# A chain of network blocks on one core: sums turned in 32x32 blocks, q's and k's parts spread in four transfers, gates as rows

## The reference

```python
scores = einsum('bqhd,bkhd->bhqk', q, k) / sqrt(8)
w = softmax(where(mask, -inf, scores), axis=-1)
return einsum('bhqk,bkhd->bqhd', w, v)
```

```python
y = sum_e gate[token, e] * (silu(x @ Wg[e]) * (x @ Wu[e])) @ Wd[e]
```

## Time and profile before

| | us |
|---|---|
| median of 3 runs | 4669.29 |
| the profiled execution, its own time | 4668.61 |
| its span in the trace | 4666.8 |
| PE busy | 4043.2 |
| DVE busy | 3448.4 |
| ACT busy | 2271.0 |

### The profile page before, as it was taken

The page is one execution under the profiler, slowest core; times in us unless marked ns, Lnnn a source line. Parts: engine busy times, 40 slices in busy tenths (PEclk is TensorE's granted clock), DMA queues, the critical chain, the costliest instruction groups (busy, mean ns, idle before and its releaser), DMA issues. The chain is left out here.

```text
span 4666.8 us, 86233 instructions
## 1 busy us (share of the span) xinstructions
PE 4043.2 (87%) x25133; PEld 2627.3 (56%) x25133; DVE 3448.4 (74%) x17477; ACT 2271.0 (49%) x7477; POOL 404.7 (9%) x338
## 2 busy tenths in 40 slices
PE   8999999999999999867888888888887346979897
PEld 6888888888888888642333333333333223534456
DVE  7888888888888888655677777776774557966543
ACT  5555555555555555424555555555555221236432
POOL 0000000000000000011111111111111010024310
PEclk9999999999999999877988888888888567989998
DMA  0000000000000000012122222222220000100001
GB/s 30 2 2 2 2 2 2 2 2 2 2 2 2 2 2 2 21 44 60 33 46 50 49 54 49 53 49 54 49 50 17 8 0 21 35 25 6 8 12 41
DMA packets 79658, 103.76 MB, mean 22 GB/s; under 512 B 25471, under 2 KB 72762, under 8 KB 77243
## 3 DMA queue, kind: packets, MB, share of 16 engines
q1 hardware_dynamic: 79227, 98.70, 8.8%
HBM read 67.60 MB, written 30.26 MB: 21 GB/s over the span
## 5 line engine op out<-in xcount | busy, mean ns | idle before, releaser
L297 DVE CUSTOM_DVE_ANT_0 I-197junk<-I-193encw,I-196expo,I-205rec 128x77 f32<-128x77 f32 x3072 | 945.6, 356 | 7.0
L1328 DVE TENSOR_REDUCE I-41263nmax<-ps 128x1 f32<-128x512 f32 x768 | 501.1, 685 | 223.7 <-PE ps L997 217.3
L1216 ACT ACTIVATE I-41266prob<-ps 128x512 f32<-128x512 f32 x768 | 428.4, 596 | 228.5 <-PE ps L1034 225.8
L275 ACT ACTIVATE I-195tanh_s<-ps 128x77 f32<-128x77 f32 x1024 | 241.3, 236 | 594.9 <-PE ps L255 594.9
L255 PEld LDWEIGHTS ps<-I-190hist,I-49small 128*128 128x128 f32 x2048 | 304.6, 188 | 298.3 <-DVE I-190hist L333 298.3
L255 PE MATMUL ps<-I-190hist,I-49small 128*128 128x77 f32 x2048 | 456.4, 304 | 0.2
L261 PE MATMUL ps<-I-195tanh_s,I-49small 128*128 128x77 f32 x2048 | 454.6, 304 | 0.0
L997 PE MATMUL ps<-I-41257kS,I-41256qS 96*128 96x512 bf16 x768 | 330.9, 457 | 130.3 <-DVE I-41263nmax L1328 58.9
L262 PE MATMUL ps<-I-190hist,I-49small 128*128 128x128 f32 x2048 | 439.5, 296 | 0.0
L257 PE MATMUL ps<-I-190hist,I-194uh_h 128*128 128x128 f32 x2048 | 439.5, 296 | 0.0
L283 ACT ACTIVATE I-201hh<-I-207gate_t,I-206pre,I-200rh 128x1 f32<-128x1 f32 x1024 | 395.5, 386 | 88.1 <-DVE I-206pre L297 0.2
(11 more groups left out here) (531 smaller groups left out, 7286.3 us busy)
## 6 DMA issues: line engine op xcount, KB each, us to landing
I-41256qS<-parts SPq DMA_DIRECT2D x24, 768.0 KB, 7.7
parts<-I-41275room SPq DMA_DIRECT2D x36, 384.0 KB, 2.5
parts<-I-41275room SPq DMA_DIRECT2D x36, 256.0 KB, 2.1
I-41257kS<-parts SPq DMA_DIRECT2D x12, 768.0 KB, 7.9
parts<-I-41275room SPq DMA_DIRECT2D x36, 128.0 KB, 1.8
I-49small<-in_layers SPq DMA_DIRECT2D x6, 768.0 KB, 8.9
I-66556w<-in_blocks SPq DMA_DIRECT2D x8, 514.0 KB, 7.5
I-41256qS<-I-41265mrow SPq DMA_DIRECT2D x192, 2.0 KB
```

The lines of the kernel that those rows point to most:

```text
L297: return e.tensor_tensor_reduce(junk[:, 2 * g + b, :], encw[:, g, b, :], expo[:, b, :], inv[:, b:b + 1], rec[:, b, g:g + 1], ALU.mult, ALU ...
L1216: e.activation(prob[:, tau % 2, j, :], k.ps[:, b, :], ACT.Exp, scale=scale).then_inc(free[b], 1)
L1328: e.tensor_reduce(nmax[:, U % HG, i, j:j + 1], k.ps[:, use[0], :], AX.X, ALU.max, negate=True).then_inc(free[use[0]], 1)
```

## The change

**Sums.** VectorE transposes `inv` in blocks of 32x32 into `wide`, which is free then; a sum that lay in a row of 32 partitions is then in a column of each block. The reciprocal takes these columns alone, 16x3 elements of a partition for groups 0 to 2 and 16x1 for the last, and writes them into the first 64 columns of `inv` (`recs`). In place of each shuffle, a transpose whose source repeats one column 32 times brings the reciprocals back over rows. Cross attention is changed in the same way. There are two more semaphores.

**Transfers.** `spread` issues four transfers for q, k and cq, one for each group of heads, each with a semaphore; ctx keeps one. TensorE waits for group m ahead of that group's first maximum. The next store waits for all four.

**Order.** `TURNS` has new strings for all five engines; the number of steps of each stream is the same.

**Gated experts.** TensorE turns the gates, so that experts are on partitions (68x1024); ScalarE copies them, and SP stores them to DRAM. For each pair SP reads two rows back, each over 64 partitions, into one of three buffers (512 KB per pair). VectorE multiplies the hidden product by this tile. The down projection then takes both experts in one product of 128 rows and sums all pairs in PSUM, in banks 4 and 5; the sum is added once at the end. The silu has two buffers, and no hardware loop is left.

In the diff, removed lines of `gated_experts` are left out (they are printed above), of `TURNS` only the beginning of GpSimd's is shown, and cross attention's part (from L1444 on), which repeats self attention's with `cinv`, `crecs` and `cwide`, is left out.

```diff
 def gated_experts(nc, k, nT, acc, gates, blocks):
     with ExitStack() as ctx:
         w = [sbuf(ctx, nc, f"w{u}", [P, 3 * P]) for u in range(GU)]
+        sil = [sbuf(ctx, nc, f"sil{u}", [P, B * T]) for u in range(2)]
         hid = [sbuf(ctx, nc, f"hid{u}", [P, B * T]) for u in range(2)]
+        spread = [sbuf(ctx, nc, f"spread{u}", [P, B * T]) for u in range(3)]
+        gT = sbuf(ctx, nc, "gT", [2 * NPAIR, B * T])
+        gates_dram = nc.dram_tensor("gates_rows", (2 * NPAIR, B * T), F32).ap()
+        gate, up, total = k.ps[:, 0:2, :], k.ps[:, 2:4, :], k.ps[:, 4:6, :]
+        turned = k.ps[0:2 * NPAIR, 6:8, :]
+        with stage(nc, "turned kept sent gate up act product hidden down summed "
+                       + " ".join(f"load{u}" for u in range(GU)) + " rows0 rows1 rows2") as (block, s):
             load = [s.load0, s.load1, s.load2, s.load3]
+            rows = [s.rows0, s.rows1, s.rows2]
             @block.sync
             def _(e):
+                def fetch(n):
                     e.dma_start(w[n % GU][:], blocks[n]).then_inc(load[n % GU], 16)
+                def fetch_rows(n):
+                    src = gates_dram[2 * n:2 * n + 2, :].unsqueeze(0).to_broadcast([64, 2, B * T])
+                    e.dma_start(spread[n % 3][0:64, :], src[:, 0, :]).then_inc(rows[n % 3], 16)
+                    e.dma_start(spread[n % 3][64:128, :], src[:, 1, :]).then_inc(rows[n % 3], 16)
+                for n in range(GU):
+                    fetch(n)
+                e.wait_ge(s.kept, B)
+                e.dma_start(gates_dram, gT[:]).then_inc(s.sent, 16)
+                e.wait_ge(s.sent, 16)
+                for n in range(3):
+                    fetch_rows(n)
+                for n in range(3, NPAIR):
+                    e.wait_ge(s.hidden, B * (n - 2))
+                    fetch_rows(n)
+                    if n + 1 >= GU and n + 1 < NPAIR:
+                        e.wait_ge(s.down, n + 2 - GU)
+                        fetch(n + 1)
             @block.tensor
             def _(e):
+                for i in range(NT):
+                    mm = e.transpose(turned[:, i // TPB, (i % TPB) * P:(i % TPB + 1) * P], gates[:, i, :], k.ident)
+                    if i % TPB == TPB - 1:
+                        mm.then_inc(s.turned, 1)
+                def hidden(n):
+                    e.wait_ge(load[n % GU], 16 * (n // GU + 1))
                     for b in range(B):
+                        if n:
+                            e.wait_ge(s.act, B * (n - 1) + b + 1)
+                        e.matmul(gate[:, b, :], w[n % GU][:, 0:P], nT[:, b * T:(b + 1) * T], start=True, stop=True).then_inc(s.gate, 1)
+                        if n:
+                            e.wait_ge(s.product, B * (n - 1) + b + 1)
+                        e.matmul(up[:, b, :], w[n % GU][:, P:2 * P], nT[:, b * T:(b + 1) * T], start=True, stop=True).then_inc(s.up, 1)
+                def down(n):
                     for b in range(B):
+                        e.wait_ge(s.hidden, B * n + b + 1)
+                        for i in range(TPB):
+                            mm = e.matmul(total[:, b, i * P:(i + 1) * P], hid[n % 2][:, b * T + i * P:b * T + (i + 1) * P],
+                                          w[n % GU][:, 2 * P:3 * P], start=(n == 0 and i == 0), stop=(n == NPAIR - 1),
+                                          skip_group_check=True)
+                    mm.then_inc(s.down, 1)
+                hidden(0)
+                for n in range(NPAIR):
+                    if n + 1 < NPAIR:
+                        hidden(n + 1)
+                    down(n)
             @block.scalar
             def _(e):
+                for b in range(B):
+                    e.wait_ge(s.turned, b + 1)
+                    e.activation(gT[:, b * T:(b + 1) * T], turned[:, b, :], ACT.Copy).then_inc(s.kept, 1)
+                for n in range(NPAIR):
                     for b in range(B):
+                        e.wait_ge(s.gate, B * n + b + 1)
+                        if n >= 2:
+                            e.wait_ge(s.product, B * (n - 2) + b + 1)
+                        e.activation(sil[n % 2][:, b * T:(b + 1) * T], gate[:, b, :], ACT.Silu).then_inc(s.act, 1)
             @block.vector
             def _(e):
+                for n in range(NPAIR):
                     for b in range(B):
+                        cols = slice(b * T, (b + 1) * T)
+                        e.wait_ge(s.up, B * n + b + 1)
+                        e.wait_ge(s.act, B * n + b + 1)
+                        if n >= 2:
+                            e.wait_ge(s.down, n - 1)
+                        e.tensor_tensor(hid[n % 2][:, cols], sil[n % 2][:, cols], up[:, b, :], ALU.mult).then_inc(s.product, 1)
                     for b in range(B):
+                        cols = slice(b * T, (b + 1) * T)
+                        e.wait_ge(rows[n % 3], 32 * (n // 3 + 1))
+                        e.wait_ge(s.product, B * n + b + 1)
+                        e.tensor_tensor(hid[n % 2][:, cols], hid[n % 2][:, cols], spread[n % 3][:, cols], ALU.mult).then_inc(s.hidden, 1)
@@ TURNS @@
-    gpsimd=("rrrrrrrrrraaarrrrrrrarrrrararrrrrrrrr", "arrrararrrrrrrrrarrrararrrrrrrrr", 3,
...
+    gpsimd=("rrrrrrrrrraaarrrrrrrrrarrarrarrrrrrrrr", "arrarrarrrrrrrrrarrarrarrrrrrrrr", 3,
...
@@ -829,6 +826,7 @@
         crow = sbuf(ctx, nc, "crow", [8, HG, T], BF16)
         cwide = sbuf(ctx, nc, "cwide", [P, 2, T])
         cinv = sbuf(ctx, nc, "cinv", [P, T])
+        recs, crecs = (x[:, 0:HG * T // 32].rearrange("p (b g) -> p b g", g=HG) for x in (inv, cinv))
         room = sbuf(ctx, nc, "room", [P, 8 * T])
         cprob = room[:, 0:4 * T].rearrange("p (j t) -> p j t", t=T)
         flat = room[:, 0:2 * T].rearrange("p (n t) -> p n t", t=T)
@@ -928,6 +926,13 @@
         K_SPOTS = (slice(2, 5), slice(1, 6, 4), slice(0, 1))
         SPOT = dict(ctx=0, cq=1, k=2, q=3)
 
+
+        def sums_of(src, lo, hi):
+            return src.rearrange("p (b q) -> p b q", q=32)[:, :, 8 + lo:8 + hi]
+
+        def along(src, g):
+            return src[:, :, g].unsqueeze(2).to_broadcast([P, T // 32, 32])
+
         def times(r, name):
             return r + 1 if name in ("k", "q") else r - 1
 
@@ -938,9 +943,9 @@
             return chain.from_iterable(part(n) for n in range(NR))
 
         with stage(nc, "full0 full1 full2 full3 full4 full5 full6 full7 free0 free1 free2 free3 free4 free5 free6 free7 "
-                       "high split av pooled inv wide normed sent0 sent1 sent2 sent3 so_in "
+                       "high split av pooled turned inv wide normed sent0 sent1 sent2 sent3 so_in "
                        "stats aggr var rstd shifted norm rotated0 rotated1 jhigh0 jhigh1 rest0 rest1 middle0 middle1 last0 last1 jstored0 jstored1 jstored2 jstored3 "
-                       "jsent0 jsent1 jsent2 jsent3 wk_ready wq_ready chigh csplit csum cinv cwide cnormed "
+                       "jsent0 cq0 cq1 cq2 cq3 k0 k1 k2 k3 q0 q1 q2 q3 wk_ready wq_ready chigh csplit csum cturned cinv cwide cnormed "
                        "csent0 csent1 csent2 csent3 wf_in wk_in wq_in") as (block, s):
             full = [s.full0, s.full1, s.full2, s.full3, s.full4, s.full5, s.full6, s.full7]
             free = [s.free0, s.free1, s.free2, s.free3, s.free4, s.free5, s.free6, s.free7]
@@ -948,7 +953,8 @@
             rotated, jhigh, rest_in, middle, last = zip((s.rotated0, s.jhigh0, s.rest0, s.middle0, s.last0),
                                                         (s.rotated1, s.jhigh1, s.rest1, s.middle1, s.last1))
             jstored = [s.jstored0, s.jstored1, s.jstored2, s.jstored3]
-            jsent = [s.jsent0, s.jsent1, s.jsent2, s.jsent3]
+
+            jsent = dict(ctx=[s.jsent0], cq=[s.cq0, s.cq1, s.cq2, s.cq3], k=[s.k0, s.k1, s.k2, s.k3], q=[s.q0, s.q1, s.q2, s.q3])
             csent = [s.csent0, s.csent1, s.csent2, s.csent3]
 
             def made(use):
@@ -989,9 +995,9 @@
                             if m and n == 2:
                                 turn(U - 1)
                                 yield
-                            if m == 0 and n == 0:
-                                e.wait_ge(s.jsent3, 16 * (a + 1))
-                                e.wait_ge(s.jsent2, 16 * (a + 1))
+                            if n == 0:
+                                e.wait_ge(jsent["q"][m], 16 * (a + 1))
+                                e.wait_ge(jsent["k"][m], 16 * (a + 1))
                             use = M["m", U, i, j]
                             b = open_bank(e, use)
                             e.matmul(k.ps[:, b, :], qS[0:ROWS_QK, c, 4 * m + j, i * P:(i + 1) * P],
@@ -1098,8 +1104,9 @@
                                 if g and i == 2:
                                     turn_cross(g - 1)
                                     yield
+                                if i == 0:
+                                    e.wait_ge(jsent["cq"][g], 16 * times(r, "cq"))
                                 if g == 0 and i == 0:
```

(24 more changed lines are left out.)

170 lines of the change are left out of this document (56 added, 114 removed).

## The result

The changed kernel took 4610.91 us (median of four runs, 4610.72 to 4613.32) where the kernel before took 4669.66 in the same comparison: 58.8 us less, ratio 0.9873 with a 95% interval of 0.9861 to 0.9885. The forecast was 4527, 142 less. The sign, the gated experts and the price of each operation came out; of the transformer's 128 us only some 42 did. The measured time lies at the edge of the wide range (4450 to 4612) and outside the forecast's own (4485 to 4575).

The account below looks back on a forecast made before the run. Dependencies, no full engine, were taken to set the transformer's period; PE and DVE nearly fill the gated experts. 4668.6 - 128.4 - 14.0 = 4526.2 us, 4527 against the median; own range 4485 to 4575, wide range 4450 to 4612.

Parts of the forecast that it names:

- the gated experts: Final stage: a pair falls from 5.61 to 5.22 us and DVE no longer trails, -14.0 us in all.
- the last group's sum: Short stretch of each transformer unit: smaller reciprocal and transposes shorten the last head group's chain, -2.3 us.
- the first unit's term: Transformer's start: the first unit's q transfer has no cover, so its earlier landing gives -5.0 us once.
- cq's landing: Before cross attention's maxima: the first of four transfers lands in 2.7 us, not 7.7, on the chain: -5.0 a unit.
- q's landing: Before self attention's maxima: q lands earlier, but normalisation is the longer chain, so costed at nothing.
- the holes: Long stretch: two cross reciprocals stop PE for 1.3 us each; their removal gives -2.6 us a unit.
- no price of its own: New order of turns, all engines: it only places the shorter work, so it was costed at nothing.
- B: Rival for the split transfers: pieces share the engines and land together, so the split does nothing; 4592, chance 0.22.
- D: Rival in the gated experts: the rows' transfers set the pair at 7.0 us; 4588, chance 0.05.
- C: Rival in the transformer's short stretch: PE's gaps close, clock stays at its upper level, -15.3 per unit; 4462, chance 0.18.
- E: Rival for the sums: block transposes are dear, up to a reciprocal's 3.35 us, making it slower; 4727, chance 0.06.
- F: Rival for the new order: an engine waits at a wrong place and the gain is lost; about 4665, chance 0.04.

Follow-up runs that it names:

- e5: Changed kernel with the old order of turns and one transfer each for k, q and cq: 4647.5 us.
- e1: Changed kernel with the order of turns of the kernel before: 4611.3 us.
- e9: Changed kernel with one transfer each for q, k and cq, and SP's queue alone in its old order: 4647.8 us.
- e7: e1 with cq's join and two remainders made on GpSimd instead of VectorE: 4595.6 us.
- f2: e5 with the next unit's first maxima put behind cq's projections in 8 of 12 units: 4653.3 us.
- g3: e1 with the next unit's first maxima put behind cq's projections in 8 of 12 units: 4643.5 us.
- e2: Kernel before with only the new order of turns: 4766.1 us.
- e8: Changed kernel (new order) with cq's join and two remainders made on GpSimd instead of VectorE: 4589.1 us.
- e4: Changed kernel (new order) with one transfer each for q, k and cq: 4674.2 us.

## Why the prediction was wrong

**Right.** The sign (0.90 on faster), the gated experts (14.0 forecast, 14.6 measured, pair 5.22 forecast and measured), the prices of the new operations, the last group's sum on the path (2.3 shorter: e5 and e1 have the projection done at 4.6 us after the attend, where before has it at 6.8 to 7.3). The first maxima start 5.0 earlier (2139.96 to 2134.92), as the first unit's term says. But most of the gain came from the ends, where I had 9.6: by the ends of attends and of the stage, the first two units gave 15.6, the next nine together 12.8, and what follows 13.6. At the middle's 1.4 a unit, some 25 of the 42 us belong to the ends; no run takes them apart.

**Wrong: cq's landing, -5.0 a unit.** I put it on the chain because the transfer starts at 2606.29 and the cross maxima at 2614.72, 8.4 us later against a landing of 7.7. That was a coincidence of two durations. The row of 2614.72 names no wait for a DMA; it follows maxima of the next unit (2612.93, 2.00 us) that had been held back by DVE. Over the whole run L1107 waited 15.1 us for that DMA (its group stands above), and in the steady part from 2459 to 3197 not once. The two were close, though: cq landed 0.3 to 1.3 us ahead of its use, so a shorter landing had nothing to win while DVE's maxima stayed where they were. The landing shrank nearly as forecast (first piece 3.4, not 2.7). e9, with cq landing 9 us ahead of its use, is no faster in its middle units, and e7, with a later cq than e1's, is faster.

**Wrong: q's landing at nothing.** The step said that normalisation "ends at the same time and is the longer chain". In the kernel before q's landing was the longer one: the transposes stood behind it in PE's queue. So the 2.3 of the sum could not count without it; together they moved the transposes by 3.5 (12.2 to 8.65 after the attend), and in the mean of the middle units the split alone moved them by 1.5 and the sum alone by 0.2. Two terms that I had set to -2.3 and 0 are one term that needs both parts: -3.5 at the transposes, of which 2.8 show in the gap of e1 (39.3 to 36.5). By f2 and g3 even that pays only while the next unit's first maxima fill the wait.

**Wrong: the holes, -2.6 a unit.** A neighbouring pair of windows is no proof that PE would fill the hole. With the reciprocals gone, PE does the same work in the same 72 us (64.87 and 64.86 us busy), so the term measured nothing. It is the new order that would have put the full reciprocals on the path (33.4 us of waiting in e2 where the kernel before has 5.2).

**Wrong: "no price of its own" for the order.** It moves cq's transfer behind a send that waits for DVE, and puts cq's work ahead of the maxima. Without the split and the turned sums it costs 94 us; with them it is worth nothing. The rows to ask were those of DVE between cq's turn and the first maximum.

**Missing: a term for DVE.** From cq's turn to the sixteenth maximum DVE is the bound of the gap (15.1 us, show its tail of ten maxima, 6.86). My chain went from cq's spread to cross maxima and left out that the scores wait for these. e8 takes 3.1 out of it and the gap shrinks by as much (35.8 to 32.7).

**Rivals.** B's mechanism (pieces land together) did not happen, its 4592 came nearest to the measured 4611 with D's 4588, by a neighbouring reason in B's case (cq's term brought nothing) and by none in D's: luck. It is luck too that 4611 still lies within the wide range, whose upper end, 4612, lies 20 us above all the mechanisms that it was made to hold. C (the clock comes back by itself) did not: it stays at 0.50 to 0.55 in the gap. D and E did not. F's wait at a wrong place is e4's, and the split hides it.

The sum with measured terms, in the middle units: gap -3.5, stretch +2.0, thus -1.5 a unit in place of -9.9. That the stretch is 1.4 longer in the new order than in the old one is moved work: PE is busy 2.3 us more in the stretch of the kernel after than in e1's, 2.1 less in the gap, and idle 0.7 less in the stretch. It has cross maxima there that stood in the gap; of the 10.0 us that it waits in all for cq's pieces, at most 2.4 fall in the middle (2443 to 3160).

## What to carry to other kernels

Before a landing is put on a path, look at the row that starts after it: if it names no wait for that DMA, an equal distance means nothing. Where an engine's queue has two waits one behind the other, shortening the one gives only what the other leaves, so price them together. A gap full of short waits is also a gap at the half clock: filling them with idle products, sized by a measured duration, gave 17 to 28 us, and moving three operations off the engine that paces the gap gave 16 to 22.

## What was not expected of the hardware

Four transfers of 192 KB on one queue land 4.6 to 4.9 us after issue in the median (q's and cq's 3.4, 4.3, 5.2 and 5.6 in their order), where one of 768 KB takes 7.7 and a single one of 192 KB 2.3; four issues cost SP 1.72 us. A float32 product of 128 columns runs as two matmuls of 0.118 us at the full clock (30 in 3.56 us). The clock fell from 1.00 to 0.50 in a single wait of 3.7 us, and was 0.55 in the mean from 2702 to 2722.
